# A selective scan beside key and value projections: two silus, two output projections and the key and value units get other slots

## The reference, cut to what matters

```python
hidden = _rmsnorm(layernorm(x), norm_w)
x, z = jnp.split(hidden @ W_in, 2, axis=-1)            # 512 -> 2 x 1024
x = jax.nn.silu(depthwise_conv4(x) + conv_b)
x_dbl = x @ W_x
dt = jax.nn.softplus(x_dbl[..., :64] @ W_dt + b_dt)
def step(h, inp):                                       # over the 224 rows
    dA = jnp.exp(dt_t[..., None] * A)                   # 1024 x 16 states
    h = dA * h + (dt_t * x_t)[..., None] * B_t[:, None, :]
    y = jnp.einsum('bdn,bn->bd', h, C_t)
y = (y + x * D) * jax.nn.silu(z)
x1 = residual + y @ W_out
kh, vh = ctx @ Wk + bk, ctx @ Wv + bv                   # 16 x 750 rows
```

## Time and profile before

| What | Before |
| --- | --- |
| median of 3 runs | 3687.46 us (3682.45 to 3690.01) |
| the profiled execution | 3689.67 us, its span 3688.3 us |
| the scans, all 512 slots | 83.7 to 1985.8 us of the span |
| one batch in the middle | 119.1 to 122.0 us |
| the last two batches | 114.2 and 103.2 us |
| DVE busy in a batch of 119.1 us | 109.5 us |
| PE busy in it | 106.2 us |
| ACT, POOL busy in it | 92.4, 94.6 us |

### The profile page before, as it was taken

How to read it: one execution, slowest core, us unless ns; L and a number is a source line. 1 busy time by engine, 2 the same in 40 slices (tenths; PEclk the granted TensorE clock), 3 DMA queues, 4 the chain that set the end, 5 groups by cost and what they waited for, 6 DMA issues and landing times. The chain is left out here.

```text
span 3688.3 us, 59573 instructions
## 1 busy us (share of the span) xinstructions
PE 3250.6 (88%) x20864; PEld 2278.9 (62%) x20864; DVE 2664.2 (72%) x4681; ACT 2377.3 (64%) x5276; POOL 1773.9 (48%) x1052
## 2 busy tenths in 40 slices
PE   5678888988898889898996799999999999789998
PEld 4556655666566656665563566666666666467887
DVE  2999999989898999889985566776766676422221
ACT  5877788677877787778863566766666666432222
POOL 2778787778877787878783000000000000035454
PEclk8799999999999999999998899999999999889999
DMA  6646756566657665666563231211211121111010
GB/s 172 185 121 178 192 164 159 158 185 181 164 139 199 182 158 153 181 188 160 143 183 101 74 90 45 82 51 45 74 58 45 50 82 46 30 54 46 23 46 23
DMA packets 286440, 425.14 MB, mean 115 GB/s; under 512 B 28641, under 2 KB 226273, under 8 KB 281538
## 3 DMA queue, kind: packets, MB, share of 16 engines
q1 hardware_dynamic: 273920, 410.75, 40.3%
q10 hardware_dynamic: 12226, 10.59, 1.0%
HBM read 320.25 MB, written 101.02 MB: 114 GB/s over the span
## 5 line engine op out<-in xcount | busy, mean ns | idle before, releaser
L704 POOL TENSOR_TENSOR a_hs<-a_rep,a_bmat 128x896 f32<-128x896 f32 x512 | 1060.2, 2092 | 327.2 <-PE a_yps L278 326.9
L603 DVE TENSOR_TENSOR_SCAN a_states<-a_states,a_hs 128x900 f32<-128x900 f32 x384 | 780.6, 2033 | 116.1 <-ACT a_states L384 111.7
L384 ACT ACTIVATE a_states<-a_rep,a_a_neg 128x224 f32<-128x224 f32 x2048 | 795.7, 438 | 69.3 <-DVE a_hs L610 66.9
L1208 DVE CUSTOM_DVE_ANT_0 b_sc<-b_sps,b_mask 112x375 f32<-112x375 f32 x1024 | 499.9, 544 | 148.3 <-PE b_sps L1019 148.0
L1035 PEld LDWEIGHTS b_tps<-b_ident,b_sc 112*125 112x125 f32 x3072 | 402.9, 191 | 279.3 <-issue 142.4
L1301 POOL TENSOR_TENSOR b_xt<-b_xt,b_bo 112x512 f32<-112x512 f32 x32 | 40.9, 1300 | 1067.9 <-DVE b_ln L1185 1067.9
L1035 PE MATMUL b_tps<-b_ident,b_sc 112*125 112x112 f32 x3072 | 492.9, 290 | 69.4 <-ACT b_sc L1126 45.3
L1126 ACT ACTIVATE b_sc<-b_sc,b_nmax 112x750 f32<-112x750 f32 x512 | 467.7, 915 | 51.9 <-DVE b_nmax L1214 51.9
L300 PE MATMUL a_work<-a_hT,w_in 128*128 128x224 f32 x2048 | 444.1, 374 | 52.4 <-ACT a_hT L416 46.1
L300 PEld LDWEIGHTS a_work<-a_hT,w_in 128*128 128x128 f32 x2048 | 410.8, 203 | 93.1 <-ACT a_hT L416 49.8
L610 DVE TENSOR_TENSOR a_hs<-a_states,a_cmat 128x896 f32<-128x896 f32 x384 | 419.0, 1091 | 13.2
(11 more groups left out here) (143 smaller groups left out, 4925.4 us busy)
## 6 DMA issues: line engine op xcount, KB each, us to landing
a_rep<-du_scratch SPq DMA_DIRECT2D x512, 224.0 KB, 5.7
w_in<-W_in_dram SPq DMA_DIRECT2D x128, 512.0 KB, 4.2
du_scratch<-a_du SPq DMA_DIRECT2D x16, 1792.0 KB, 10.9
ctx<-ctxT_dram SPq DMA_DIRECT2D x48, 500.0 KB, 5.2
v_scratch<-kv_out SPq DMA_DIRECT2D x96, 250.0 KB
k_scratch<-kv_out SPq DMA_DIRECT2D x96, 250.0 KB, 4.0
b_keys<-k_scratch SPq DMA_DIRECT2D x16, 1500.0 KB, 11.7
b_v<-v_scratch SPq DMA_DIRECT2D x16, 1500.0 KB
```

The source lines that it names most:

```text
L384: e = act.activation(rows(states[:, g % DA, :])[:, q, 1:ROW], rep[tile % REPS][:, j, 0, :], ACT.Exp, scale=a_neg[:, g % SLOTS, q:q + 1])
L603: dve.tensor_tensor_scan(state if g % G4 else whole, state, whole, 0.0, ALU.mult, ALU.add).then_inc(S["scan"], 1)
L704: pool.tensor_tensor(hs[g % RING][:, :, 1:ROW], rep[tile % REPS][:, j, 1, :].unsqueeze(1).broadcast_to([P, Q, L]), bmat[b % 2][:], ALU.mul ...
L1208: dve.tensor_tensor_reduce(out=sc[block % 2][:, j, cols], in0=sps[0:TT, j, 0:HALF], in1=mask[:, block % 2, cols], scale=-1.0, scalar=3.0e3 ...
```

## The change

It moves steps between slots and computes nothing else. In windows of 32 slots it has 11 key and value units in place of 12; 9 of the others go to slots 16 to 31 of batch 0, and 2 more to each of the last two windows (20 in place of 18). For them the loads of Wk, Wv and the first context go from SP's slot 16 to slot 6 of batch 0. The silu of z goes from slot 19 to 20, the two `logs` steps of the softplus (L495, L497) from slots 10, 12, 14, 16 to 9, 11, 13, 15. The first output projection goes from slot 11 to 12, behind the last raw dt step. The residual is added three slots behind a projection (slots 15 and 17) in place of two (13 and 16). The statistics of x1 go from slot 20 to 19, those of the rows from 3 to 4.

```diff
-    O_SLOTS = (39 + BEHIND, 42 + BEHIND)
+    O_SLOTS = (40 + BEHIND, 42 + BEHIND)
...
         LATER = {
-            "load": [-68], "row_stats": [-65], "squares": [-60], "guess": [-58], "gains": [-54], "h": [-53], "hT": [-51],
+            "load": [-68], "row_stats": [-64], "squares": [-60], "guess": [-58], "gains": [-54], "h": [-53], "hT": [-51],
...
-            "series": spaced(-28, 2), "logs": spaced(-26, 2), "skip": [-20, -19], "spread": [-19], "dt_sum": [-18],
-            "silu_z": [-17], "u": [-16], "store_du": [-15]}
+            "series": spaced(-28, 2), "logs": spaced(-27, 2), "skip": [-20, -19], "spread": [-19], "dt_sum": [-18],
+            "silu_z": [-16], "u": [-16], "store_du": [-15]}
...
-        usual = (1, 3, 5, 9, 12, 16, 18, 20, 22, 24, 26, 31)
-        last_but_one = (1, 3, 5, 9, 12, 14, 15, 16, 18, 19, 20, 22, 23, 24, 26, 27, 28, 30)
-        last = (-1, 1, 2, 3, 5, 6, 8, 9, 12, 13, 14, 16, 17, 18, 20, 21, 22, 24)
-        kv_slot = ([w * SLOTS + BEHIND + at for w in range(1, B - 2) for at in usual]
+        first = (16, 17, 18, 22, 24, 26, 28, 30, 31)
+        usual = (1, 3, 5, 12, 14, 18, 20, 22, 24, 26, 31)
+        last_but_one = (1, 3, 5, 12, 13, 14, 15, 16, 17, 18, 19, 20, 21, 22, 23, 24, 26, 28, 29, 30)
+        last = (-1, 1, 2, 3, 5, 6, 7, 12, 13, 14, 15, 16, 17, 18, 19, 20, 21, 22, 23, 24)
+        kv_slot = ([*first] + [w * SLOTS + BEHIND + at for w in range(1, B - 2) for at in usual]
                    + [(B - 2) * SLOTS + BEHIND + at for at in last_but_one] + [(B - 1) * SLOTS + BEHIND + at for at in last])
...
                 for b in range(B):
                     at = slot - b * SLOTS
-                    if at - 2 in O_SLOTS:
-                        add_residual(b, O_SLOTS.index(at - 2))
-                    if at == O_SLOTS[1] + 6:
+                    if at - 3 in O_SLOTS:
+                        add_residual(b, O_SLOTS.index(at - 3))
+                    if at == O_SLOTS[1] + 5:
                         x1_stats(b)
...
-                    if slot == b * SLOTS + O_SLOTS[1] + 3:
+                    if slot == b * SLOTS + O_SLOTS[1] + 4:
                         store_x1(b)
...
-                if slot == SLOTS // 2:
+                if slot == 6:
                     for dst, src in ((wk, t["Wk"]), (wv, t["Wv"])):
```

## The result

The changed kernel takes **3648.88 us** (median of 4 runs, 3648.29 to 3652.70) where the kernel before takes 3688.74 (4 runs, 3682.45 to 3690.32). The ratio is 0.9897, with a 95% interval of 0.988 to 0.9914. The forecast of 3634 was too low by 15 us. The direction held, and so did the range of 3615 to 3650, by 1.1 us. The profiled execution of after has a span of 3646.9 us, where that of before has 3688.3, so 41.4 us are to be accounted for.

What follows compares the result with a forecast made beforehand. DVE's order of work was taken to set the period. 71 us won over 13 batches, less 2.6 (start), 13.8 (end) and 1 (copy buffers), gave 53.6: 3636 us profiled, 3634 as median, range 3615 to 3650.

Steps and rivals of the forecast that it cites:

- What bounds the kernel: Middle batches: DVE's order of work sets the period; its idle time, 9.65 of 119.1 us, is what moving slots can win.
- Slots 22 to 4: PE starts a unit ahead and keeps its lead to slot 3; waits at slots 25, 29, 1 go, 2.8 us a batch.
- the lead is not kept: Rival from slot 22 on: PE runs at its 14.7 us, waits at 25, 29, 1 stay; 3670 us, chance 0.10.
- Slots 19 to 22: The silu of z is hidden by taps and a scan; the scan of slot 22 comes 1.5 us sooner a batch.
- the late silu still stalls: Rival at slot 22: the projection onto x runs at low clock, the scan waits 1.75 us; 3657 us, chance 0.10.
- Slots 11 to 19: PE idles 6.5 us, loses 2.2 to low clock; the scan of slot 19 comes 0.7 later, behind about 2 us of wait.
- the 48 to 52 that I gave: Sign: the forecast is wrong unless the scan of slot 19 starts 48 to 52 us after slot 5's; before, 49.2.
- Batches of 122 us: Low clock from the idle time before slot 20 no longer reaches DVE: 1.2 us a batch, 120.3 less 119.1.
- The ends: Cost of moved units: 2.6 us at the start in batch 0, 13.8 in the last two batches, 1 for copy buffers.
- The sum: Whole kernel: 5.5 us a batch times 13 is 71 us, less 2.6, 13.8 and 1, leaves 53.6 us won.

Runs made afterwards that it cites:

- Silu back: The changed kernel with the silu of z back in slot 19 and the statistics of x1 back in slot 20: 3689.84 us, ratio 1.0006 to the kernel before.
- Unit at slot 11: The changed kernel with the unit of slot 16 moved to slot 11 in the middle windows: 3608.69 us, ratio 0.9788 to the kernel before.
- logs back: The changed kernel with the logs of the softplus back in slots 10, 12, 14 and 16: 3632.72 us, ratio 0.9863 to the kernel before.
- units back: The changed kernel with the old key and value unit tables and loads, every other edit kept: 3681.50 us, ratio 0.9982 to the kernel before.
- start and end: Against the kernel with twelve units a window (3593.04 us): 8 units in batch 0, 14 in the last window, none between its output projections: 3593.89 us.
- logs back, unit at 11: The changed kernel with the unit of slot 16 in slot 11 and the softplus logs back in slots 10, 12, 14, 16: 3616.26 us, ratio 0.9809.

## Why the prediction was right and where it was off

**What bounds the kernel.** Right. DVE's work in 13 batches fell by 0.5 us each (1421.64 to 1414.87 us); the other 3.9 of the 4.4 us won are its gap.

**Slots 22 to 4, forecast 2.8 a batch.** Right in mechanism and size: the waits at 25, 29 and 1 went, nothing took their place, and in batch 9 the stretch from the scan of slot 22 to that of slot 5 takes 52.48 us in place of 55.64, 3.2 won. The rival "the lead is not kept" is out. Silu back shows how thin this is: a late slot 21 brings the wait of slot 1 back.

**Slots 19 to 22.** Right: the silu is hidden to 0.27 us. The rival "the late silu still stalls" is out; the projection onto x took 3.19 us at the full clock. The trace again has no drain behind the table loads (1216.15 + 1.28, the next instruction at 1217.45).

**Slots 11 to 19: the step that was mis-sized.** The chain is the one that I described: 6.18 us of idle PE, low clock, sums, dt, projections, sums of slot 16, unit, copy, decays. Its loss to the clock, though, was 3.9 us where I took 2.2 and allowed 2.8 at most: 1.5 in the sums, 0.8 in the dt step, 1.6 in the projections. It reached the unit's end after 25.6 us, not 24.1. So from the scan of slot 5 to that of slot 22 batch 9 takes 63.43 us against 63.48 before: 0.05 won, 1.5 forecast, 19 us over 13 batches. I had taken a value between two rows, though the longer idle time of the two, 5.54 us, was nearer to the 6.5 that I forecast, and no row bounded the loss behind a longer one. Unit at slot 11 shows the term by itself: 13.90, 1.02 and 1.74 us at the full clock. The rest of the chain was sized right: 25.6 less 3.9 is 21.7 us, where I had 21.9. The loss itself isn't given by the idle time alone: in 5 of the 13 batches of silu back and in all of logs back the same chain lost less. So it did in the first of the 13 batches of after, with 3.19, 1.02 and 13.90 us, and that batch took 113.5 us.

The wait itself also had another form than forecast. I put it at about 2 us ahead of the scan of slot 19. It came as 2.3 to 2.5 us at add_y, which needs PE's sums of slot 16, 0.2 at slot 18, and 1.1 to 1.3 ahead of the scan of slot 19, 3.6 to 4 us in all. I had followed PE's chain to the unit and ACT's copy, and not asked who waits for the sums in the middle of it. The scan of slot 19 starts 51.2 us after that of slot 5, inside the 48 to 52 that I gave, 1.3 later than my sum.

**Batches of 122 us, forecast 1.2.** Right: the sums of slot 20, slow in the long batches of before (3.22 us in those of 122.0, 1.74 in batch 9), take 1.74 in all batches of after. After three at the start of 113.5, 116.6 and 116.2, its batches take 115.9 to 116.3.

**The ends.** The last two batches cost 15.1 us, 14.8 forecast. The start cost 4.9 in place of 2.6. In batch 1 DVE waits 1.10 us at the scan of slot 1 and 2.67 at L619 for PE's sums of slot 0. Every kernel with units in slots 30 and 31 of batch 0 has these two waits, within 0.02 us; before, units back, and start and end (8 units, none behind slot 28) have neither. So the late units cost 3.8 us, where I had put 2.6 for all nine; the other 1.1 came within batch 0. Units back starts 3.4 us late for other reasons: its first scan begins 1.35 us later, and DVE waits 2.76 us in place of 1.27 at the scan of slot 11 of batch 0, ahead of any unit.

**The sum.** With the middle 13.5 us lower, the start 2.3, the end 0.3, and 3.9 us from the phases behind that are no part of the change, the forecast of 53.6 becomes the 41.4 measured in the spans. That the result fell inside the range is in part luck: it is 1.1 us below the upper end, and those 3.9 us, which stand in the two profiled executions and which nobody forecast, are more than that. The range allowed a loss of 2.8 us at most in the chain, and the loss was 3.9.

**Which part did it.** In the presence of the others the unit tables are worth 3.5 us a batch, the silu with the statistics 2.9, and the moved output projections -0.8. The row statistics are worth nothing. The earlier logs cost 1.6 us a batch in the changed kernel, where the clock stayed low longer with them, and saved 0.8 with the unit at slot 11, where without them it fell ahead of slot 20. The parts overlap, so these don't add to 4.4. The ends take back 20 of the 57.5 us, and twelve units a window with one of them at slot 11 don't need the payment at the end: 56 us below after.

## What to carry to other kernels

When independent work is thinned out, ask where the thinned engine then stands idle ahead of a chain that others wait for, and leave one piece there: a 3.7 us unit moved from the chain's end into the gap ahead of it was worth as much as the whole change. Follow a late engine not only to the last reader of its chain but to each reader on the way. And before work is paid for at the ends of a loop, try whether the middle can hold it in another slot; here the twelfth unit cost the middle nothing, 112.78 us a batch with it and without.

## What the runs showed of the hardware

- The low clock behind like idle times did not last alike. In batch 9 of after, with 6.18 us of idle, the granted clock was 0.50 (1.2 GHz) for 10.25 us, from inside the idle time through sums, dt step and the start of the projections. With the logs back and 6.54 us of idle, the sums took 3.02 us but dt step and projections had the full clock. In silu back both cases come in one execution. The one run of logs back at a mean clock of 0.942 took 3653.5 us, against 3629.5 to 3634.8 at 0.952 and 0.953: 20 us from one order of instructions. One run of such a kernel isn't enough to judge a small edit by.
- Filling the idle time at slot 11 did not by itself bring the clock back for the sums. Behind 4.79 us of the small filler matmuls the sums still took 3.07 us; behind a value unit of 5.39 us, or a key unit of 5.33 in the batches beside it, they took 1.74. Both stood behind some 3.1 to 3.5 us of idle time. Which difference between the two kinds of work matters, no run here shows.
- Ahead of the sums of slot 20 the clock fell in 5 of 13 batches of logs back, unit at 11, behind 2.2 to 3.1 us of idle. In the other 8, behind 3.0 to 3.3 us, it did not, nor in any batch of unit at slot 11, behind 1.9 us. The length of the idle time alone does not tell whether it falls.
- Many kernels here settle into batch periods that repeat by turns: 115.9 and 116.2 us in after, 111.8 and 113.4 with twelve units, and, counted from slot 22, 113.3 and 115.4 with the logs back. A small edit can shift which of them occur, so a few us of difference between near kernels need not belong to the edit.
